# Rows by SyncE for five tiles a head, a re-ordered start and another last part in a graph and memory kernel

## The chip, the cores and the metric

The kernel runs on one core of one Trainium2 chip. The metric is device microseconds (us) of one execution. The engines are TensorE (PE in the profile, its weight loads PEld), VectorE (DVE), ScalarE (ACT), GpSimd (POOL) and SyncE (SP); they run side by side and meet at semaphores.

## The reference

Input is x (2048 x 128) and a symmetric adjacency matrix (2048 x 2048). Four blocks follow each other, each on the layer-normalised x and added to it:

```
x = x + hyperbolic_graph_attention(norm(x), adj)      # dense masked softmax over 2048 neighbours
x = x + lns_linear(norm(x))                           # sign(x w) * |x| @ |w| + bias
x = x + graph_attention(norm(x), adj)                 # the second attention: leaky scores, elu
x = x + product_key_memory_attention(norm(x))         # 8 heads
```

The last block takes most of the time. For each of the 8 heads and each of the 2048 rows: two queries of 64 are compared with 128 keys each, the best 16 of each are combined to the best 16 of their sums, and these 16 numbers pick 16 rows of a table of 8 x 16384 rows (a key and a value of 128 floats each, so 1 KB a row). The 16 rows are summed with softmax weights: k and v of that row. Then comes causal attention over the 2048 rows, softmax(q k^T) v, and a projection added to x:

```
k = einsum(kv_scores, keys_table[ind]); v = einsum(kv_scores, values_table[ind])
attn = softmax(where(causal, q @ k.T, -max)); out = (attn @ v) @ Wo
```

All of it is float32.

## The kernel before

The 2048 rows are 16 tiles of 128. The three first blocks are done by about 340 us; their last part, the second attention, ends in five groups of tiles, GROUPS = (0,2), (2,6), (6,10), (10,14), (14,16). Of each group VectorE makes the ELU (elu_in and elu_out, with ScalarE's elu_exp between), adds it to x and takes the variance, ScalarE the root (norm_root), VectorE the normalising factors (normal), ScalarE the normalised rows (rows_in), TensorE their transposes (group), ScalarE their copy to aT (group_out). Before the change groups 3 and 4 end after TensorE's sum of tile 0 of head 0, and ScalarE does elu_exp(3) and all the rest of the two groups behind kv_out(0), the copy of that sum. Only then come project(5), scores(0) and step 1.

The memory block is a loop over heads (0, a hardware loop for 1 to 6, and 7) and in it over steps t = 0 to 15. Work of several tiles is in flight in a step:

- VectorE finds the 16 best of tile t+4 (find_start to look_up_5; the row numbers go to `rows`, rows_full), spreads the weights of tile t+1 to 16 diagonal matrices (spread, line 792), takes the maxima of tile t-1's scores (score_max, L799) and adds tile t-2's projected output to x (add_out, L807 and L812).
- GpSimd gathers tile by tile (gather, L321): one indirect DMA for each k of 0 to 15, which brings one table row to each of 128 partitions, into slot t % 4 of `ring`. Before a tile it waits for rows_full and for slot_free (L319), which ScalarE gives when the tile four before is summed (L1175).
- SyncE fetches the sixteenth rows (k = 15) of the tiles for which by_rows holds; GpSimd then issues 15 gathers for such a tile. The row numbers are transposed by TensorE (turn_offsets), scaled and copied by ScalarE (offsets_out) to `offs`, and SyncE loads them to registers 32 at a time (L268) and issues 128 DMAs of 1 KB (L272). Before, these are tiles 3, 7, 11, 15 (without 3 in head 0), and the offsets of tile t+3 are turned in step t.
- TensorE, in step t: project(t+5) (L1589 to L1593), the offsets, sums(t) (L1565: 16 products of a diagonal matrix with 128 x 256 gathered rows, waiting for four landings at a time), then values(t-1) (L1628 transposes of the probabilities, L1641 products with v, L1658 projection), turn_keys(t) (L1597) and scores(t) (L1610 past columns, L1616 and L1617 own columns).
- ScalarE makes the exponentials of the scores (softmax, L1248), copies transposed probabilities (L1259), sums (L1177), keys (L1268) and outputs (L1263).

Each engine's order is written out by hand; there is no planner. In the last step of head 7 the kernel before splits tile 15's sum around the first scores (sums(..., (0,)), then (1, 2), then the last quarter inside values(14)), has the maximum in two parts (L943, L946), and ends with softmax(15) over 2048 columns and values(15). The last addition is L954, and SyncE copies the last three tiles out.

## Time and profile before

| what | us |
|---|---|
| median of 3 runs | 2843.3 |
| lowest and highest of them | 2838.46, 2846.46 |
| the profiled execution, its own time | 2838.24 |
| its span, first to last instruction | 2836.3 |
| mean granted TensorE clock in it | 0.932 of full |

The profile is of one execution. Times in a timeline are us from the start of the span; a row is a start, a duration, the engine, the line, the operation, what it writes and reads, and in square brackets how long the engine sat idle before it and what ended that. DVEq, ACTq, PEq and POOLq are the engines' queues, here waits on semaphores. "issue" means that nothing in the profile shows a wait.

### The profile page before, as it was taken

The page shows a single profiled execution, that of the slowest core. Times are in us where ns is not written, and L with a number is a line of the kernel's source. Part 1 is how long each engine was busy: PE and PEld are TensorE (multiplying, and loading weights), DVE is VectorE, ACT ScalarE, POOL GpSimd, SP SyncE. Part 2 cuts the span into 40 slices and gives each one's busy share as a digit, 9 for nine tenths or more (in the row PEclk, how much of TensorE's full clock was granted, in tenths as well). Part 3 has the DMA queues.
Part 4 walks back from the last instruction along what each step waited for, and adds up shares of the span by engine and source line. Part 5 has one row for each costly group of instructions (what it writes and reads, how often), then busy time and mean ns, then how long its engine had stood idle before and what let it go on. Part 6 is the DMA issues. An engine that isn't in the chain of part 4 may idle for free. (4 is left out here: it accounts for less than half of the span.)

```text
span 2836.3 us, 47902 instructions
## 1 busy us (share of the span) xinstructions
PE 2195.5 (77%) x11489; PEld 1773.8 (63%) x11489; DVE 1867.1 (66%) x6336; ACT 783.3 (28%) x2063; POOL 1931.2 (68%) x2033
## 2 busy tenths in 40 slices
PE   6948678887788777886878767877788777877777
PEld 6948556766566556665666655665566655665565
DVE  6689777766666666657566665656666666666541
ACT  5746422221122212221222212221223112221222
POOL 0003767777777777777777777777777777777773
PEclk8969889999999899999899899998999989989999
DMA  4301333333333333333333333333333333333332
GB/s 154 108 1 30 91 95 108 111 108 108 107 111 108 109 108 111 107 108 109 107 110 109 109 107 111 109 110 107 108 110 108 109 108 110 108 109 107 107 108 74
DMA packets 116173, 293.47 MB, mean 103 GB/s; under 512 B 37600, under 2 KB 49248, under 8 KB 113792
## 3 DMA queue, kind: packets, MB, share of 16 engines
q0 software_dynamic: 96816, 264.50, 32.6%
q1 hardware_dynamic: 14880, 23.22, 2.5%
q10 hardware_dynamic: 4144, 2.17, 0.3%
q8 instruction: 105, 1.72, 0.3%
q14 instruction: 228, 1.87, 0.2%
HBM read 288.69 MB, written 1.05 MB: 102 GB/s over the span
## 5 line engine op out<-in xcount | busy, mean ns | idle before, releaser
L321 POOL DMA_INDIRECT ring<-table,rows x2017 | 1923.6, 954 | 707.4 <-issue 578.3
L1565 PE MATMUL ps<-ring,staged 128*128 128x256 f32 x4096 | 995.8, 400 | 191.0 <-DMA ring<-table,rows 169.8
L1565 PEld LDWEIGHTS ps<-ring,staged 128*128 128x128 f32 x4096 | 806.0, 200 | 355.4 <-DMA ring<-table,rows 212.1
L807 DVE RECIPROCAL prec<-psum_row 128x1 f32<-128x1 f32 x128 | 21.0, 164 | 502.1 <-DVEq L806 501.8
L1641 PE MATMUL ps<-s2w,work 128*128 128x128 f32 x2176 | 306.2, 288 | 34.6 <-PEq L1639 33.8
L1177 ACT ACTIVATE work<-ps 128x256 f32<-128x256 f32 x128 | 49.0, 383 | 978.6 <-ACTq L1175 978.6
L1641 PEld LDWEIGHTS ps<-s2w,work 128*128 128x128 f32 x2176 | 274.3, 198 | 64.7 <-issue 61.2
L1610 PE MATMUL ps<-work,qT 128*128 128x512 f32 (+3 forms) x576 | 242.8, 552 | 70.4 <-PEq L1602 67.0
L799 DVE TENSOR_REDUCE nmax<-ps 128x1 f32<-128x128 f32 (+7 forms) x127 | 162.7, 1281 | 204.2 <-DVEq L798 203.5
L792 DVE TENSOR_TENSOR staged<-ps,wgt 128x2048 f32<-128x2048 f32 x128 | 292.0, 2281 | 0.2 <-issue 0.2
L1628 PE MATMUL ps<-ident,work 128*128 128x128 f32 x1088 | 189.8, 298 | 41.9 <-PEq L1551 21.7
L1610 PEld LDWEIGHTS ps<-work,qT 128*128 128x128 f32 x576 | 102.8, 195 | 178.8 <-issue 178.8
L1259 ACT ACTIVATE s2w<-ps 128x512 f32<-128x512 f32 (+2 forms) x320 | 169.4, 533 | 133.6 <-ACTq L1258 132.1
L1628 PEld LDWEIGHTS ps<-ident,work 128*128 128x128 f32 x1088 | 144.0, 154 | 79.1 <-issue 67.6
L1248 ACT ACTIVATE work<-ps,nmax 128x128 f32<-128x128 f32 (+15 forms) x128 | 148.3, 1158 | 39.2 <-ACTq L1246 34.7
L1593 PE MATMUL ps<-keyd,qpk 128*128 128x256 f32 x246 | 88.6, 444 | 88.9 <-PEq L1592 88.9
L762 DVE TENSOR_TENSOR pick<-bposf,ps 128x864 f32<-128x864 f32 x128 | 135.0, 1054 | 9.8 <-issue 0.4
L766 DVE TENSOR_TENSOR pick<-pick,ps 128x864 f32<-128x864 f32 x128 | 135.0, 1055 | 9.6
L1418 PE MATMUL ps<-work 128*128 128x128 f32 x1024 | 137.5, 279 | 4.1 <-PEq L1415 4.0
L1418 PEld LDWEIGHTS ps<-work 128*128 128x128 f32 x1024 | 126.7, 195 | 6.2 <-issue 6.0
L1658 PE MATMUL ps<-wo,oT 128*128 128x128 f32 x256 | 60.1, 317 | 87.3 <-PEq L1657 87.3
L1238 ACT ACTIVATE qpk<-ps 128x128 f32<-128x128 f32 x123 | 34.1, 277 | 333.1 <-ACTq L1237 333.1
(246 smaller groups left out, 2583.3 us busy)
## 6 DMA issues: line engine op xcount, KB each, us to landing
ring<-table SPq DMA_DIRECT2D x3968, 1.0 KB
ring<-table,rows POOLq DMA_INDIRECT x2017, 2.7
staged<-adj_in SPq DMA_DIRECT2D x16, 1024.0 KB, 4.8
xs<-x_in SPq DMA_DIRECT2D x4, 256.0 KB, 6.6
wpkq<-w_pkq ACTq DMA_DIRECT2D x7, 128.0 KB
out<-xs SPq DMA_DIRECT2D x1, 832.0 KB, 4.8
keyd<-pk_keys ACTq DMA_DIRECT2D x14, 32.0 KB
wo<-w_o ACTq DMA_DIRECT2D x7, 64.0 KB, 2.0
```

The lines of the kernel that those rows point to most:

```text
L321: nc.gpsimd.indirect_dma_start(ring[:, t % RING, k, :], None, table_d, bass.IndirectOffsetOnAxis(ap=rows[:, t % ROWS, k:k + 1], axis=0),). ...
L762: v.tensor_tensor(pick[:, :, :], bposf[:, :].unsqueeze(2).to_broadcast([P, TOPK, NCAND]), iota_ps.unsqueeze(1).to_broadcast([P, TOPK, NCAN ...
L766: v.tensor_tensor(pick[:, :, :], pick[:, :, :], cand_ps.unsqueeze(1).to_broadcast([P, TOPK, NCAND]), ALU.mult)
L792: v.tensor_tensor(diag(t), ident_ps.unsqueeze(1).to_broadcast([P, TOPK, P]), wgt[:, t % 4, :].unsqueeze(2).to_broadcast([P, TOPK, P]), ALU ...
L799: v.reduce_max(nmax[:, t % 2:t % 2 + 1], ps[:, 4:8, :].rearrange("p b n -> p (b n)")[:, 0:(t + 1) * P], X, negate=True).then_inc(nmax_full, 1)
L1248: s.activation(prob[:, t % 2, 0:L], ps[:, 4:8, :].rearrange("p b n -> p (b n)")[:, 0:L], ACT.Exp, bias=nmax[:, t % 2:t % 2 + 1], accum_out ...
L1259: s.activation(pts[:, (parity + b) % 2, 0:n * P], ps[:, 2 + (parity + b) % 2, 0:n * P], ACT.Copy).then_inc(pt_sb, 1)
L1418: ins = m.matmul(ps[:, OUT_BANKS[layer][t % banks], 0:D], ptg[:, n % 3, i * P:(i + 1) * P], hB[:, j, :], start=(j == 0), stop=(j == T - 1))
L1565: ins = m.matmul(to, diag(t)[:, k, :], ring[:, t % RING, k, :], start=(k == 0), stop=(k == TOPK - 1))
L1610: ins = m.matmul(ps[:, 4 + at // 512, 0:w], qT[:, t % 8, :], kT[:, at:at + w], start=True, stop=True)
L1628: ins = m.transpose(ps[:, 2 + (parity + b) % 2, j % 4 * P:(j % 4 + 1) * P], prob[:, t % 2, j * P:(j + 1) * P], ident[:, :])
L1641: ins = m.matmul(ps[:, 1, 0:P], kv[:, j, D:2 * D], pts[:, (parity + b) % 2, j % 4 * P:(j % 4 + 1) * P], start=(j == 0), stop=(j == t))
```

## The change

- by_rows: tiles 1, 4, 7, 10, 13 of each head (in head 0 only those above 4: 7, 10, 13). The offsets have three buffers, and the landings three semaphores, taken in turn. The offsets of tile a are turned in step a-3, as before. Tile 15's sixteenth row is a gather with a semaphore of its own.
- Opening: ScalarE does elu_exp(3) and exp_best(3) ahead of kv_out(0), then project_out(5) and key_out(0), and the rest of groups 3 and 4 after these. TensorE does project(5), turn_keys(0), scores(0) ahead of group(3), group(4). VectorE does find_halves(4) and then elu_out(3), find_all(4), and has spread(1) ahead of elu_out(4). Step 0 of head 0 is written out so.
- End of head 7: TensorE's loop stops at tile 13. Tiles 14 and 15 are summed by VectorE (weighted), row by row as the quarters land, with the running sum in PSUM. Row 15's softmax has two parts: columns 0 to 1919 with their own maximum, summed and projected as an output of its own, and the 128 own columns with the overall maximum; the first part is scaled by exp of the difference of the two maxima. The outputs are copied out in three parts: tiles 0 to 13, 14, 15.

The core of the diff:

```
-LOADED = 32
+LOADS = ((0, 32), (32, 64), (64, 96), (96, P))
+BY_ROWS = (1, 4, 7, 10, 13)
+def turned_at(t, first, last):
+    a = t + AHEAD - 1
+    return by_rows(a % T, first and a < T) and not (last and a >= T)
 def by_rows(t, first):
-    return t % RING == RING - 1 and not (first and t == RING - 1)
+    return t in BY_ROWS and not (first and t <= AHEAD)
+def buffer_of(t):
+    return BY_ROWS.index(t) % 3
...
-            def fetch_rows():
+            def fetch_rows(t):
+                for lo, hi in LOADS:
                     _, at = nc.values_load_multi_w_load_instructions(
-                        offs[0:1, c:c + LOADED], engines=(mybir.EngineType.SP,), min_val=0, max_val=(HEADS * NKV - 1) * ROW_BYTES,
+                        offs[0:1, buffer_of(t), lo:hi], engines=(mybir.EngineType.SP,), min_val=0, max_val=(HEADS * NKV - 1) * ROW_BYTES,
                         skip_runtime_bounds_check_because="row numbers are sums of a head's offset and two positions")
-                    for i in range(LOADED):
-                        sp.dma_start(ring[c + i:c + i + 1, RING - 1, TOPK - 1, :].bitcast(U8),
-                                     table_bytes[:, bass.ds(at[i], ROW_BYTES)]).then_inc(rows_in_sem, 16)
+                    for i in range(lo, hi):
+                        sp.dma_start(ring[i:i + 1, t % RING, TOPK - 1, :].bitcast(U8),
+                                     table_bytes[:, bass.ds(at[i - lo], ROW_BYTES)]).then_inc(copied_in[buffer_of(t)], 16)
...
+                    ).then_inc(last_in if t == T - 1 and k == TOPK - 1 else gathered[t % RING][k // QK], 16)
...
+            spread(1)
+            elu_out(4)
             weigh(AHEAD - 1)
...
+            def weighted(t, q):
+                landed(t, q)
+                for k in range(q * QK, (q + 1) * QK):
+                    w, row = wgt[:, t % 4, k:k + 1], ring[:, t % RING, k, :]
+                    if t == T - 1 and k == TOPK - 1:
+                        dve.wait_ge(last_in, 16 * HEADS)
+                    if k == 0:
+                        v.tensor_scalar(end_ps, row, w, None, ALU.mult)
+                    elif k < TOPK - 1:
+                        v.scalar_tensor_tensor(end_ps, row, w, end_ps, ALU.mult, ALU.add)
+                    else:
+                        v.scalar_tensor_tensor(kv[:, t, :], row, w, end_ps, ALU.mult, ALU.add).then_inc(kv_full, 1)
+                    v.drain()
+            def add_out(t):
+                add_out_1(t)
+                v.drain()
+                add_out_2(t)
+                v.drain()
+            for t in range(T - 2):
                 step(t, False, True)
+            add_out(T - 4)
+            weighted(T - 2, 0)
+            score_max(T - 3)
+            for q in range(1, QUARTERS):
+                weighted(T - 2, q)
+            score_max(T - 2)
+            add_out(T - 3)
+            dve.sem_inc(out_ready, 1)
+            weighted(T - 1, 0)
             dve.wait_ge(s_full, 1)
             dve.sem_inc(s_full, -1)
-            v.reduce_max(npart[:, 0:1], ps[:, 4:7, :].rearrange("p b n -> p (b n)"), X, negate=True)
+            v.reduce_max(max_past, ps[:, 4:8, :].rearrange("p b n -> p (b n)")[:, 0:(T - 1) * P], X,
+                         negate=True).then_inc(nmax_full, 1)
+            weighted(T - 1, 1)
+            weighted(T - 1, 2)
+            add_out(T - 2)
+            dve.sem_inc(out_ready, 1)
+            weighted(T - 1, 3)
             dve.wait_ge(s_full, 1)
             dve.sem_inc(s_full, -1)
-            v.reduce_max(npart[:, 1:2], ps[:, 7, :], X, negate=True)
+            v.reduce_max(max_own, ps[:, 7, 3 * P:4 * P], X, negate=True)
             v.drain()
-            v.tensor_tensor(nmax[:, 1:2], npart[:, 0:1], npart[:, 1:2], ALU.min).then_inc(nmax_full, 1)
-            add_out_1(T - 2)
+            v.tensor_tensor(max_all, max_past, max_own, ALU.min).then_inc(nmax_full, 1)
+            dve.wait_ge(scales_ok, 1)
+            v.scalar_tensor_tensor(denom, sum_past, old_scale, sum_own, ALU.mult, ALU.add)
             v.drain()
-            add_out_2(T - 2)
-            add_out_1(T - 1)
+            v.reciprocal(f_own, denom)
             v.drain()
-            v.scalar_tensor_tensor(xs[:, T - 1, :], ps[:, 1, P:2 * P], prec[:, 3:4], xs[:, T - 1, :],
+            v.tensor_tensor(f_past, f_own, old_scale, ALU.mult)
+            v.drain()
+            dve.wait_ge(proj_full, 1)
+            dve.sem_inc(proj_full, -1)
+            v.scalar_tensor_tensor(xs[:, T - 1, :], ps[:, 1, P:2 * P], f_past, xs[:, T - 1, :], ALU.mult, ALU.add)
+            v.drain()
+            dve.wait_ge(proj_full, 1)
+            dve.sem_inc(proj_full, -1)
+            v.scalar_tensor_tensor(xs[:, T - 1, :], ps[:, 0, P:2 * P], f_own, xs[:, T - 1, :],
                                    ALU.mult, ALU.add).then_inc(out_ready, 1)
...
+            def last_steps():
+                t = T - 1
+                past = t * P
+                row = prob[:, t % 2, :]
+                scored = ps[:, 4:8, :].rearrange("p b n -> p (b n)")
+                softmax(t - 2)
+                turned_out(t - 2, PARITY[t - 2], t - 1)
+                softmax(t - 1)
+                turned_block(t - 1, PARITY[t - 1], 0)
+                turned_block(t - 1, PARITY[t - 1], 1)
+                act.wait_ge(nmax_full, 1)
+                act.sem_inc(nmax_full, -1)
+                s.activation(row[:, 0:past], scored[:, 0:past], ACT.Exp, bias=max_past, accum_out=sum_past).then_inc(prob_full, 1)
+                turned_block(t - 1, PARITY[t - 1], 2)
+                turned_block(t - 1, PARITY[t - 1], 3)
+                output_turned()
+                for b in range(4):
+                    turned_block(t - 1, PARITY[t], b)
+                key_out(t, ps[:, 0, 2 * P:3 * P])
+                output_turned()
+                act.wait_ge(nmax_full, 1)
+                act.sem_inc(nmax_full, -1)
+                s.activation(row[:, past:N], scored[:, past:N], ACT.Exp, bias=max_all, accum_out=sum_own).then_inc(prob_full, 1)
+                s.activation(old_scale, max_past, ACT.Exp, scale=-1.0, bias=max_all).then_inc(scales_ok, 1)
+                act.wait_ge(pt_full, 1)
+                act.sem_inc(pt_full, -1)
+                s.activation(ptown[:, :], ps[:, 0, 3 * P:4 * P], ACT.Copy).then_inc(pt_sb, 1)
+                output_turned(oTown, ps[:, 0, 0:P])
...
+            project_out(AHEAD + 1)
+            key_out(0)
+            norm_root(*GROUPS[3])
+            rows_in(3)
+            elu_exp(4)
+            group_out(3)
+            norm_root(*GROUPS[4])
+            rows_in(4)
+            group_out(4)
+            for t in range(1, T):
...
+            def last_steps():
+                t = T - 2
+                exponentials()
+                past_scores(t)
+                values(t - 1, PARITY[t - 1], bank1, key=t)
+                t = T - 1
+                exponentials()
+                past_scores(t).then_inc(s_full, 1)
+                values(t - 1, PARITY[t - 1], bank1)
+                exponentials()
+                turn_block(t - 1, PARITY[t], 0, t)
+                bank1()
+                for b in range(3):
+                    turn_block(t - 1, PARITY[t], b + 1, t)
+                    sum_block(t - 1, PARITY[t], b)
+                kv_copied()
+                turn_keys(t, ps[:, 0, 2 * P:3 * P])
+                sum_block(t - 1, PARITY[t], 3).then_inc(ot_full, 1)
+                pe.wait_ge(kt_sb, 1)
+                pe.sem_inc(kt_sb, -1)
+                own_scores(t)
+                output(t)
+                exponentials()
+                m.transpose(ps[:, 0, 3 * P:4 * P], prob[:, t % 2, t * P:N], ident[:, :]).then_inc(pt_full, 1)
+                pe.wait_ge(pt_sb, 1)
+                pe.sem_inc(pt_sb, -1)
+                m.matmul(ps[:, 0, 0:P], kv[:, t, D:2 * D], ptown[:, :], start=True, stop=True).then_inc(ot_full, 1)
+                pe.wait_ge(ot_sb, 1)
+                pe.sem_inc(ot_sb, -1)
+                m.matmul(ps[:, 0, P:2 * P], oTown[:, :], wo[:, :], start=True, stop=True).then_inc(proj_full, 1)
...
+            project(AHEAD + 1)
+            kv_copied()
+            turn_keys(0)
+            scores(0)
+            group(3)
+            group(4)
+            pe.wait_ge(bank7_free, 1)
+            pe.sem_inc(bank7_free, -1)
+            for t in range(1, T):
```

## Rows read from the trace of the kernel before

**Rows 1.** The page, busy us (share of the span) and instructions
```profile
PE 2195.5 (77%) x11489; PEld 1773.8 (63%) x11489; DVE 1867.1 (66%) x6336; ACT 783.3 (28%) x2063; POOL 1931.2 (68%) x2033
```
**Rows 2.** Line L321: engine, operation, durations, first and last start
```profile
L321 POOL DMA_INDIRECT ring<-table,rows x2017: 940/946/2411, 255.6 to 2801.6; - x184
...
DMA to landing us min/median/max: 2.6/2.7/5.0
```
**Rows 3.** Timeline, GpSimd: start, duration, instruction, idle before
```profile
371.87 0.95 POOL L321 DMA_INDIRECT ring<-table,rows  x1 [0.30 <-issue]
...
380.83 0.94 POOL L321 DMA_INDIRECT ring<-table,rows  x1 [8.02 <-POOLq L319]
...
2801.59 0.94 POOL L321 DMA_INDIRECT ring<-table,rows  x1 [0.30 <-issue]
```
**Rows 4.** Timeline of the opening, all engines
```profile
331.71 9.39 PE L1565 MATMUL ps<-ring,staged 128*128 128x256 f32 x32 [3.86 <-PEq L1558]
...
342.36 0.69 DVE L583 SCALAR_TENSOR_TENSOR fin<-fin,work 128x512 f32<-128x512 f32 x1 [7.44 <-DVEq L345]
...
351.91 0.17 DVE L779 CAST rows<-rowf 128x16 uint32<-128x16 f32 x1
...
355.09 1.09 PE L1459 MATMUL ps<-ident,work 128*128 128x128 f32 x4 [13.99 <-PEq L1457]
...
362.32 0.66 PE L1459 MATMUL ps<-ident,work 128*128 128x128 f32 x2 [6.14 <-PEq L1457]
...
367.73 0.30 DVE L710 MAX8 half<-sim 128x8 f32<-128x128 f32 x1 [0.88 <-DVEq L708]
...
368.79 0.64 PE L1589 MATMUL ps<-aT,wpkq 128*128 128x128 f32 x2
...
371.56 8.19 PE L1565 MATMUL ps<-ring,staged 128*128 128x256 f32 x32
...
379.76 0.17 DVE L779 CAST rows<-rowf 128x16 uint32<-128x16 f32 x1
...
379.95 0.38 ACT L1177 ACTIVATE work<-ps 128x256 f32<-128x256 f32 x1 [7.32 <-ACTq L1175]
```
**Rows 5.** SyncE: line L268, and one fetch in the timeline
```profile
L268 SPq TENSOR_LOAD <-offs x124: 2025/2124/2153, 413.3 to 2775.4; - x124
...
934.92 48.30 SPq L272 DMA_DIRECT2D ring<-table  x128
```
**Rows 6.** Windows: stretch, length, busy us, granted clock, DMA share, GB/s
```profile
500.00:1500.00 1000.00, 791.20 (x3914) 625.66 (x3915) 657.68 (x2318) 238.07 (x664) 756.21 (x801) 0.95 0.38 109
```
**Rows 7.** Timeline of the end, all engines
```profile
2765.65 1.99 PE L1565 MATMUL ps<-ring,staged 128*128 128x256 f32 x8 [1.36 <-DMA ring<-table,rows]
...
2778.05 2.02 DVE L799 TENSOR_REDUCE nmax<-ps 128x1 f32<-128x1792 f32 x1 [3.55 <-DVEq L798]
...
2795.81 3.25 PE L1610 MATMUL ps<-work,qT 128*128 128x512 f32 x8 [0.56 <-PEq L1602]
...
2799.65 2.16 DVE L799 TENSOR_REDUCE nmax<-ps 128x1 f32<-128x1920 f32 x1 [3.76 <-DVEq L798]
...
2801.94 1.86 ACT L1248 ACTIVATE work<-ps,nmax 128x1920 f32<-128x1920 f32 x1 [6.27 <-ACTq L1246]
...
2804.03 5.16 PE L1610 MATMUL ps<-work,qT 128*128 128x512 f32 x8 [2.81 <-PEq L1621]
...
2818.44 0.30 PE L1597 MATMUL ps<-ident,work 128*128 128x128 f32 x1 [0.74 <-PEq L1551]
...
2819.29 0.46 PE L1616 MATMUL ps<-causal,ident 128*128 128x128 f32 x2 [0.55 <-PEq L1649]
...
2825.59 1.06 PE L1628 MATMUL ps<-ident,work 128*128 128x128 f32 x8 [1.49 <-PEq L1621]
...
2832.12 0.28 ACT L1263 ACTIVATE oT<-ps 128x128 f32<-128x128 f32 x1 [1.41 <-ACTq L1262]
...
2833.39 0.35 DVE L954 SCALAR_TENSOR_TENSOR xs<-ps,prec,xs 128x128 f32<-128x128 f32 x1
```

More of the change, by code:

```diff
@@ L835, in step @@
                 a = (t + AHEAD) % T
-                begun = not (first and t == 0)
-                find = begun and not (last and t >= T - AHEAD)
+                find = not (last and t >= T - AHEAD)
                 out = not (first and t < 2)
-                weigh = begun and not (last and t >= T - AHEAD + 1)
+                weigh = not (last and t >= T - AHEAD + 1)
                 if t == T - AHEAD and find:
@@ L853, in step @@
                     find_second(a)
-                if begun:
-                    score_max((t - 1) % T)
-                if not (last and t == T - 1):
+                score_max((t - 1) % T)
+                if not (last and t == T - 3):
                     spread((t + 1) % T)
@@ L938, in _, with landed, per @@
                     step(t, False, False)
-            for t in range(T):
-                step(t, False, True)
+            def landed(t, q):
+                def per(first):
+                    return [16 * (QK - (q == QUARTERS - 1 and (s == T - 1 or by_rows(s, first)))) for s in range(t % RING, T, RING)]
+                dve.wait_ge(gathered[t % RING][q], (HEADS - 2) * sum(per(False)) + sum(per(True)) + sum(per(False)[:t // RING + 1]))
+            def weighted(t, q):
[11 more added lines that the diff above has]
+                    v.drain()
@@ L1315, in _ @@
                     step(h, t, False, False)
-            for t in range(T):
+            for t in range(T - 2):
                 step(HEADS - 1, t, False, True)
-            softmax(T - 1)
-            turned_out(T - 1, PARITY[T - 1])
+            last_steps()
         @block.tensor
@@ L1537, in per @@
                 def per(first):
-                    return [16 * (QK - (q == QUARTERS - 1 and by_rows(s, first))) for s in range(t % RING, T, RING)]
+                    return [16 * (QK - (q == QUARTERS - 1 and (s == T - 1 or by_rows(s, first)))) for s in range(t % RING, T, RING)]
                 if first:
@@ L1572, in _ @@
             bank1()
-            sums(0, 0, range(QUARTERS), True)
-            group(3)
-            group(4)
-            pe.wait_ge(bank7_free, 1)
-            pe.sem_inc(bank7_free, -1)
+            sums(0, 0, True)
             def project(t):
@@ L1668, in step @@
                     project((t + AHEAD + 1) % T)
-                if t % RING == 0 and not (first and t == 0):
+                if turned_at(t, first, last):
                     turn_offsets()
-                if first and t == 0:
-                    kv_copied()
-                    turn_keys(0)
-                    scores(0)
-                    return
-                if last and t == T - 1:
-                    sums(h, t, (0,), False, end_ps)
-                    exponentials()
-                    past_scores(t).then_inc(s_full, 1)
-                    sums(h, t, (1, 2), False, end_ps)
-                    values(t - 1, PARITY[t - 1], bank1, t)
-                    return
                 if t == 0:
@@ L1687, in step @@
                     bank1()
-                    sums(h, 0, range(QUARTERS), False)
+                    sums(h, 0, False)
                     kv_copied()
@@ L1692, in step @@
                         bank1()
-                    sums(h, t, range(QUARTERS), first)
+                    sums(h, t, first)
                     exponentials()
```

173 lines of the change are left out of this document (85 added, 88 removed).

## Prediction

> **What bounds the kernel now.** I read the busy shares first, then the largest group, then its instructions in order of time, then the two ends of that stretch. The busy shares [rows 1] name no engine: TensorE 77%, GpSimd 68%, VectorE 66%. The group of gathers [rows 2] is the one to follow: 2017 of them, one every 1.25 us (0.95 busy, 0.30 before the next), from 255.6 to 2801.6 us. In order of time [rows 3], gather 80 starts at 371.87, gather 81 at 380.83 after 8.02 us of waiting, and the last at 2801.59. From the 81st to the last are 1936 steps in 2420.76 us, 1.2504 us each, so GpSimd never waits there: that stretch is its queue and nothing else, whatever the other engines do. TensorE's waits inside it are waits for gathers. So the time has three parts: the opening up to gather 81, the stretch at 1.25 us per gather, and the end from the last gather on (2801.59 to 2836.3), which is a chain over TensorE, ScalarE and VectorE [rows 7]. The DMA engines are at a share of 0.38 [rows 6], so issuing, not moving, sets the 1.25.
>
> **Part 1, rows fetched by SyncE.** Before, head 0 has 3 tiles of which the sixteenth row goes by SyncE (7, 11, 15), the other seven 4 each: 31. After, head 0 has 7, 10, 13, the others 1, 4, 7, 10, 13: 3 + 35 = 38. So 7 gathers less: 7 x 1.2504 = 8.75 us, if GpSimd stays the bound. All removed ones lie behind gather 81. The cover: SyncE needs 48.3 us for its 128 copies with three loads of row numbers between, and 2.1 us for the first load [rows 5], 50.4 us. Before, a fetch comes every 63 gathers, 79 us; after, 3 tiles apart, 47 gathers, 58.8 us, so 8 us are left. Five fetches are 252 us of a head of 251 gathers, 313.9 us. The fetch of tile a still starts in step a-3 and is wanted after the last quarter of tile a; between lie about 62 gathers less the 12 us by which that step starts late (tile 13's scores end 12 us after its last quarter starts [rows 7]), 65 us against 50.4 plus the landing. At tile 4 it is tight, because TensorE comes out of a head's first step late and catches up: there it may wait a few us, but the ring holds four tiles, 60 us of gathers, so GpSimd doesn't notice. Bounds: 0 (something else takes over) and 8.75; I take 8.75. The added order of offsets (a buffer of three, one transpose and one copy per fetch, as before) makes 7 more of each on engines with idle time: nothing.
>
> By the Trainium skill (DMA: Bandwidth & Descriptors, "Issuing engines are not separate DMA queues") DMAs of all engines end on the same 16 DMA engines, and issuing from several saves only the issuing engine's time; were the transfers the bound, this part would give 0 and the sum 20.3 instead of 29. This case's trace shows issue as the bound: even steps at a share of 0.38.
>
> **Part 2, the opening.** Gather 81 is tile 5's first. It wants tile 5's row numbers (VectorE ends them at 379.93) and slot 1, free when tile 1 is summed (ScalarE copies it at 379.95) [rows 4]: both are late, and equally. Both go back to one place. TensorE ends tile 0's sum at 341.1 and then sits 13.99 us until VectorE and ScalarE have group 3's normalised rows, does group 4 at 362.32, and only then project(5), scores(0), project(6) (368.79) and tile 1's sum (371.56 to 379.75). VectorE in turn had waited 7.44 us for ScalarE's exponential of group 3, queued behind the copy of tile 0's sum; from there to tile 4's row numbers took it 342.36 to 352.08, 9.7 us. After the change that exponential is ahead of the copy, so these 9.7 us start when the halves of tile 4 are searched, about 335.0 (an estimate: tile 0's spread ends near 331.7, and the search takes some 3 us), and end at 344.8. TensorE does project(5) and scores(0) at once, by about 345.6 (two copies and four products at the 0.4 us that each takes with its handover [rows 7], 4.5 us), and ScalarE then turns to group 3's root. From tile 4's row numbers to group 3's transposes were 3.2 us (351.91 to 355.09), so these come at 348.0 to 348.8; from group 3's to group 4's 7.2, now with spread(1) between but done while ScalarE writes group 3's rows: 355.2 to 356.0. The copy takes 0.85 with its handovers, project(6) 2.8 and tile 1's sum 8.2 to 9.4: slot 1 is free at 367.9 to 369.1. VectorE enters step 1 when group 4's rows are normalised, about 354.5, and ends tile 5's row numbers 12.2 us later (367.73 to 379.93 before), 366.7. GpSimd wants both at 371.87 + 1.25 = 373.1. The wait goes with 4 us to spare: 8.96 - 1.25 = 7.71 us. What is late next: tile 6, wanted 20 us later at 393, with TensorE's step of about 14 us behind 369; later tiles have more room. Bounds 0 and 7.71; I take 7.71.
>
> Together the last gather starts at 2801.59 - 8.75 - 7.71 = 2785.13.
>
> **Part 3, the end.** I count from the start of the last gather. Before, the last VectorE operation ends at 2833.74, that is at +32.15 [rows 7]. After, tiles 14 and 15 are no longer summed by TensorE, so nothing waits for their last gathers but VectorE, which adds 16 rows of 256 columns one after another. The nearest row is the same operation over 128 columns, 0.35 us; 128 more columns at about 1 ns (the reductions: 2.16 - 2.02 = 0.14 us for 128) make 0.49, with 0.07 between, 0.56 us, and 2.2 us a quarter (between 1.4 and 4).
> The chain starts with tile 13's scores. Tile 13 has 15 gathers now and tile 15 has 16, and the wait of 1.36 us before its last quarter goes, so its row maximum starts at -24.9 instead of -23.5. From there:
> maximum 2.0; softmax 1.75 (1.86 over 1920 columns) with its accumulator and two handovers, 2.2; scores of row 14 over 14 tiles. These take 3.0 at the full clock (3.25 x 14/15), but TensorE has then idled 4.2 us; before, it idled 2.8 us and the 3.25 us of work took 5.16. So 4.9, reached at -15.8. Two blocks of row 13's values, 3.7 (16 tiles take 6.5 from the first transpose to the copy of the result, 0.41 a tile, and the start of the first); tile 14's keys and own scores 1.8, to -10.3; the sum of tile 14 is ready at -15.0 (last landing -17.2, then 2.2), in time. Rest of row 13's values and the copy 3.4, softmax 14 2.1, scores of row 15 3.4: to -1.4. Maximum of 1920 columns 2.2, its exponential 2.2 to +3.0. This exponential stands on ScalarE before the last two blocks of row 14, so these end late: copies, sums, copy and projection to 6.9. Then 15 tiles of row 15's values: 6.7, to 13.6. Own scores 0.7, to 14.3, and from there ten short operations in a row (maximum, minimum, exponential, its partner, transpose, copy, product, copy, projection, last addition) at 0.43 to 0.5 (a transpose and a copy take 0.85 from start to start of the next), 4.6: +18.9. Tile 15's sum is no part of it: VectorE does its last quarter behind add_out(14), at 7.6 to 9.8, wanted at 12.4.
> The exponential in the middle gives TensorE another idle of about 1.3 us (2.9 if it slips), which the trace doesn't price alone: between 0 and 1.9 us more. I take 0.7: +19.6. Gain 32.15 - 19.6 = 12.5 us, between 8 (every idle costs 1.9, VectorE at 1 us per row) and 15.
> The Trainium skill (TensorE: Matmul & The Clock Gate, "HAM oscillation") says that idle gaps between bursts put TensorE back to the lower clock, which speaks against taking sums off TensorE here. The trace agrees: 5.16 us against 3.25 after the 2.81 us gap. With no such drop the forecast would be 2.6 us lower.
>
> **The sum.** Last operation at 2785.13 + 19.6 = 2804.7. The last copy out and what follows took 2836.3 - 2833.74 = 2.56: span 2807.3. The profiled execution's own time is 1.94 over its span: 2809.2, 29.0 us (1.0%) under its 2838.24. That execution is 5.1 under the median of the runs; I take 29.0 off the median: 2814.3.
>
> **Rivals.**
> A. The opening's wait stays or comes back at tile 6 or 7, because VectorE and ScalarE in the new order trail by more than the 4 us to spare. For it: both releasers of gather 81 must move, through some ten handovers. Against: both have room. Price 7.7: 2822. Chance 0.12.
> B. The end gives half or less: TensorE at the lower clock through the chain, or the exponential over 1920 columns in the middle pushing two more waits. Price 6 to 9: 2822. Chance 0.17.
> C. Other side: SyncE becomes the bound. It is then busy 80% of a head, with 8 us between fetches where it had 28. The point where it decides is a fetch of 313.9 / 5 = 62.8 us; every us above costs 35 us (5 x 7). At 65 us: 77 us over, so 2814 + 77 = 2891; slower than before from 63.6. For it: its copies already follow each other without a gap (128 in 48.3 us, loads included). Against: nothing of this burst depends on how often it comes, and the DMA engines have room. Chance 0.04.
> D. The seven gathers bring nothing, because the bytes are the same and the DMA engines, or TensorE waiting for rows at tile 4 in each head, set the pace. Against: a DMA share of 0.38, and 60 us of ring. Price 8.75: 2823. Chance 0.05.
> The forecast itself 0.62.
>
> **The numbers.** 2814, range 2804 to 2828: the low end is the end's best (15) and a run at the lower edge of the three shown, the upper A or D with B's lower price (2814 + 7.7 + 6 = 2828). A measurement of this kernel tells about 0.3%, 8.5 us, from no change. All cases but C are over that; a mixture of A, B and D at their worst (25 us) is what lands within it. Faster 0.94, same 0.02, slower 0.04.
>
> **What would show it.** 2010 gathers; no wait of GpSimd of a microsecond or more from gather 36 on, the 81st at 373.1; the last starting at 2785; its pace still 1.25; SyncE's bursts still 48 us, about 10 apart. At the end: no sum of tile 14 or 15 on TensorE in head 7, row 13's maximum 25 us before the last gather, a granted clock of half in row 14's scores, the last VectorE operation 19 to 20 us behind the last gather. The forecast is wrong if GpSimd shows waits inside the stretch, or if the last operation is over 24 us behind the last gather.

## The result, and the profile after

The changed kernel takes 2813.39 us (median of four runs, 2812.64 to 2815.2) where the kernel before takes 2842.07 (2838.46 to 2846.46): a ratio of 0.9899 with a 95% interval from 0.9882 to 0.9917. The prediction was 2814. The profiled execution took 2812.64 us, with a span of 2810.8.

The page of the changed kernel, busy us with the share of the span [rows 1]:

```profile
PE 2187.1 (78%) x11434; PEld 1761.3 (63%) x11434; DVE 1878.3 (67%) x6369; ACT 785.3 (28%) x2073; POOL 1930.2 (69%) x2026
```

Its gathers (now line L340), and what their engine waited for, in us and times [rows 2]:

```profile
L340 POOL DMA_INDIRECT ring<-table,rows x2010: 945/949/2422, 254.9 to 2790.7; - x183
  issue: 577.2, 1892
  POOLq L338: 116.6, 100
```

Seven gathers fewer. L338 is the wait for a slot of the ring. The timeline of GpSimd around the gather that had waited 8.02 us [rows 3], and its last gather:

```profile
372.78 0.95 POOL L340 DMA_INDIRECT ring<-table,rows  x1 [0.31 <-issue]
...
2790.74 0.95 POOL L340 DMA_INDIRECT ring<-table,rows  x1 [0.30 <-issue]
```

Gather 81 starts at 372.78 without a wait (forecast 373.1). But 2790.74 is 5.6 us later than the forecast 2785.13: 1929 steps in 2417.96 us are 1.2535 each, not the 1.2504 of before, which is 6.0 us. The pace is the same while SyncE copies and while it doesn't (1.2535 and 1.2534), and the duration of one gather is up by the same 3 ns: median 949 against 946 [rows 2].

The end of the changed kernel in the timeline, all engines [rows 7], in which the last gather starts at 2790.74:

```profile
2765.80 2.02 DVE L818 TENSOR_REDUCE nmax<-ps 128x1 f32<-128x1792 f32 x1 [1.28 <-DVEq L817]
2767.74 4.42 DVE L969 SCALAR_TENSOR_TENSOR ps<-ring,wgt,ps 128x256 f32<-128x256 f32 x8
2769.94 5.52 PE L1701 MATMUL ps<-work,qT 128*128 128x512 f32 x8 [4.29 <-PEq L1712]
...
2785.43 3.46 PE L1701 MATMUL ps<-work,qT 128*128 128x512 f32 x8 [1.38 <-PEq L1712]
...
2789.03 2.16 DVE L993 TENSOR_REDUCE tail<-ps 128x1 f32<-128x1920 f32 x1 [1.94 <-DVEq L992]
2791.32 1.86 ACT L1348 ACTIVATE work<-ps,tail 128x1920 f32<-128x1920 f32 x1 [0.78 <-ACTq L1347]
...
2799.60 0.48 DVE L971 SCALAR_TENSOR_TENSOR work<-ring,wgt,ps 128x256 f32<-128x256 f32 x1
2801.86 0.27 PE L1688 MATMUL ps<-ident,work 128*128 128x128 f32 x1
...
2807.53 0.35 DVE L1018 SCALAR_TENSOR_TENSOR xs<-ps,tail,xs 128x128 f32<-128x128 f32 x1 [1.46 <-DVEq L1017]
```

From the last gather to the end of the last VectorE operation are 17.14 us, where before had 32.15 and the forecast 19.6. A row added on VectorE takes 0.49 us with 0.07 before the next (eight take 4.42). Tile 15's sum is ready at 2800.08 and wanted at 2801.86, so it hides, with 1.8 us to spare. The span of 2810.8 is the forecast 2807.3, plus 5.6 for the pace, less 2.5 for the end, and 0.4 in the last copy out.

### The profile page after: what moved, and what is told of

The parts are those of the page before. It is cut to its first block and busy times, and to the rows that moved or that the text cites. A ratio compares the mean times of both kernels' runs of the same rounds, so it can differ in the third digit from the quotient of the medians.

```text
span 2810.8 us, 49771 instructions
## 1 busy us (share of the span) xinstructions
PE 2187.1 (78%) x11434; PEld 1761.3 (63%) x11434; DVE 1878.3 (67%) x6369; ACT 785.3 (28%) x2073; POOL 1930.2 (69%) x2026
## 3 DMA queue, kind: packets, MB, share of 16 engines
HBM read 288.69 MB, written 1.05 MB: 103 GB/s over the span
## 5 line engine op out<-in xcount | busy, mean ns | idle before, releaser
L340 POOL DMA_INDIRECT ring<-table,rows x2010 | 1922.6, 957 | 699.3 <-issue 577.2
L1309 ACT ACTIVATE work<-ps,nmax 128x128 f32<-128x128 f32 (+7 forms) x127 | 146.1, 1151 | 22.2 <-ACTq L1307 21.5
```

The costliest lines, as they stand in the source:

```text
L340: nc.gpsimd.indirect_dma_start(ring[:, t % RING, k, :], None, table_d, bass.IndirectOffsetOnAxis(ap=rows[:, t % ROWS, k:k + 1], axis=0),). ...
L1309: s.activation(prob[:, t % 2, 0:L], ps[:, 4:8, :].rearrange("p b n -> p (b n)")[:, 0:L], ACT.Exp, bias=nmax[:, t % 2:t % 2 + 1], accum_out ...
```

## The experiments

Kernels of one group ran on one chip beside the kernel before. In the first and the third group everything ran in a slow condition of the machine (the kernel before at 4200 and 4108 us instead of 2836), in which a change of one per cent can't be judged, and the decisive kernels of the first were run again in the second.

**First group: the kernel before and the changed one again, and two parts undone.** b_again and a_again have no edit. u1_four has four fetched tiles a head, four tiles apart as before, though not the same ones (before: 3, 7, 11, 15):

```
-BY_ROWS = (1, 4, 7, 10, 13)
+BY_ROWS = (1, 5, 9, 13)
```

u2_open has the old order of the opening on all three engines and everything else new; TensorE's part of it:

```
             group(3)
+            group(4)
...
-            project(AHEAD + 1)
-            kv_copied()
-            turn_keys(0)
-            scores(0)
-            group(4)
+            project(AHEAD + 1)
+            kv_copied()
+            turn_keys(0)
+            scores(0)
```

> The kernel before, once more, for its pace only. Between gather 81 and the last its gathers were 1.2504 us apart, those of the changed kernel 1.2535, which cost that one 6.0 us of the 8.75 that seven gathers less should bring. Theory A (the pace is the chip's and the execution's, not the kernel's): before and after have the same pace here, within 0.001, whatever it is. Theory B (SyncE's seven further fetches slow every gather): before again 1.2504, after again 1.2535.

> The changed kernel, once more. Theory A: the same pace as before in this call, within 0.001; the last gather then starts 16.1 us before the one of before (8.75 + 7.71, less the 0.4 that its first gathers differ), and the time is 31 to 32 us under before. Theory B: 1.2535 against 1.2504, and 28 to 29 us under. Both: last VectorE operation 17.1 us behind the last gather's start.

> The changed kernel with four tiles a head by SyncE (1, 5, 9, 13), three in head 0: 2017 gathers as before, the rest as changed. Theory A: 8.75 us slower than the changed kernel, same pace as it. Theory B: seven gathers more but each 0.0031 us faster: 2.8 us slower only, pace 1.2504.

> The changed kernel with the opening of before (groups 3 and 4 ahead of project(5) and scores(0), ScalarE's exponential of group 3 behind the copy of tile 0's sum, spread(1) last). Both theories: gather 81 waits some 8 us again, everything behind it 7.7 us later, time 7.7 us over the changed kernel. If the wait was going to be made good later (rival: work that the ring's four slots hide anyway), under 2 us.

Measured: before 4199.62 us (4176.14 to 4208.09), b_again 4190.19. a_again 4482.67, ratio 1.0672 [1.0618, 1.0727]; u1_four 4291.82, 1.0239 [1.0189, 1.0288]; u2_open 4505.25, 1.0728 [1.0672, 1.0783]. None of the times expected came: the change is 6.7% slower here, and with four fetches a head instead of five it is slower by 4.3 points less. What did come is theory A of b_again: where gathers follow each other without a wait they are 1.2502 us apart in b_again and 1.2501 in a_again. So the changed kernel isn't what made the pace 1.2535 in its first profile. The waits of GpSimd in a_again, in us, times and the longest:

```profile
POOL ring L340 <- POOLq L338: 1748.6, 126, 84.2
POOL ring L340 <- issue: 574.7, 1884, 0.9
```

The issue row is as ever, the other 1632 us more than in the first profile: GpSimd is no longer the bound. Nor is it in the kernel before, where this wait is 1327.2 us in b_again. SyncE's copies in a_again (ns min/median/max):

```profile
L289 SPq DMA_DIRECT2D ring<-table x4864: 2/228/1436, 467.6 to 4424.5; - x195
```

The median copy takes what it takes otherwise, but some take 1.4 us, and the 128 copies of a fetch come to some 77 us alone and 98 us when three fetches follow each other (294 us for three), against 48.7. The kernel before has the same long ones (maximum 1421 ns), and its other engines stand too, at fixed lines: the wait before one VectorE operation, which is 9.4 us in the first profile of before, in b_again:

```profile
L752 DVE MAX8 best<-candr 128x8 f32<-128x54 f32 x128 | 27.9, 218 | 357.6 <-issue 355.5
```

Nothing that the profile shows releases these waits. What causes them I can't settle.

How far SyncE holds up the rest can be read from TensorE's wait for the fetched sixteenth row, on the semaphore of the copies (L1661, in the kernel before L1564; us, times, longest), in a_third of the second group (undisturbed), in b_again, u1_four, a_again, and in c1_all and s7_seven of the third group (six and seven fetches a head):

```profile
PE ps L1662 <- PEq L1661: 2.7, 2, 2.1
...
PE ps L1565 <- PEq L1564: 161.3, 10, 24.0
...
PE ps L1662 <- PEq L1661: 200.5, 12, 25.3
...
PE ps L1662 <- PEq L1661: 319.1, 15, 25.2
...
PE ps L1662 <- PEq L1661: 567.0, 24, 40.8
...
PE ps L1662 <- PEq L1661: 1036.8, 45, 43.1
```

In the slow condition TensorE waits for rows of SyncE already before the change, and 158 us more in the changed kernel, of the 303 us by which the span of a_again (4491.5) is over b_again's (4188.2). With seven fetches it waits 875 us more, and the span of 4991.5 is 803 over b_again's, 886 over the median of before in its own group (4105.5).

**Second group: the same comparison undisturbed.** a_third is the changed kernel, u1_four_b and u2_open_b are u1_four and u2_open. u3_end has the new rows and opening with the old end: TensorE sums tiles 14 and 15 (in parts, as before), row 15's maximum has two parts and its exponential is one over 2048 columns, and tile 15's sixteenth row is a gather. Its edit is the end of three engines and the two last copies out put back; the core:

```
-            add_out(T - 4)
-            weighted(T - 2, 0)
-            score_max(T - 3)
...
-            weighted(T - 1, 3)
+            v.reduce_max(npart[:, 0:1], ps[:, 4:7, :].rearrange("p b n -> p (b n)"), X, negate=True)
...
+            v.reduce_max(npart[:, 1:2], ps[:, 7, :], X, negate=True)
```

> The changed kernel once more, since the chip of the first call ran every kernel at 4180 us and more: there SyncE took 98 us for the 128 copies of a fetch instead of 48, over the 62.8 us from which the prediction's rival C has it decide. Theory A (C's rule: the changed kernel wins where a fetch stays under 62.8 us and loses where it doesn't): fetches of 48 to 49 us go with 28 to 32 us under before, fetches of about 98 us with 5 to 8% over it. Theory B (the second chip slows the changed kernel for another reason): the sign doesn't follow the length of a fetch.

> The changed kernel with four tiles a head by SyncE (1, 5, 9, 13), three in head 0: 2017 gathers. Where a fetch takes 48 us: 8.75 us slower than the changed kernel if the pace per gather is the chip's (theory A), 2.8 us if seven fetches more had slowed every gather from 1.2504 to 1.2535 (theory B). Where a fetch takes 98 us: 4 to 5% faster than the changed kernel.

> The changed kernel with the opening of before. Where a fetch takes 48 us: gather 81 waits some 8 us, everything behind it comes 7.7 us later, 7.7 us over the changed kernel; rival (made good later): under 2 us. Where a fetch takes 98 us: within 0.5% of the changed kernel, since GpSimd isn't the bound there.

> The changed kernel with the end of before (TensorE sums tiles 14 and 15, row 15's softmax in one part over 2048 columns), tile 15's sixteenth row still a gather of GpSimd. Where a fetch takes 48 us: 13 to 16 us slower than the changed kernel (its last operation came 17.1 us behind the last gather's start, before's 32.1, and one gather more stands at the end here); rival (the gain of the end came from the idle chip and not from the order): under 6 us. Same last gather start as the changed kernel in both theories.

Measured, beside the kernel before at 2835.64 us (2835.04 to 2839.65, seven runs):

| kernel | us | ratio, 95% | gathers | gather 81 | last gather | end of last operation behind it |
|---|---|---|---|---|---|---|
| a_third | 2806.95 | 0.9894, 0.9877 to 0.9910 | 2010 | 373.83 | 2785.75 | 17.69 |
| u1_four_b | 2814.80 | 0.9922, 0.9905 to 0.9938 | 2017 | 372.78 | 2793.62 | 17.50 |
| u2_open_b | 2817.31 | 0.9930, 0.9913 to 0.9946 | 2010 | 381.39 | 2793.44 | 19.70 |
| u3_end | 2818.78 | 0.9937, 0.9920 to 0.9953 | 2010 | 373.85 | 2785.82 | 27.98 |

The time of each kernel over a_third is what the part is worth: 7.85 us for the seven gathers, 10.4 for the opening, 11.8 for the end. Their sum is 30.0, against the whole change's 28.7: the parts add up to within 1.3 us. The 11.8 are under the 13 to 16 that were expected of u3_end, which had been counted from before's 32.1 and the 17.1 of the first profile of the changed kernel; they are well over the rival's 6. In the two profiles u3_end is 10.3 us longer behind its last gather, and the rest is in the copies out and between executions. In u1_four_b gather 81 happens to start 1.05 earlier, and from there it has 1936 steps to a_third's 1929, 8.9 us more. The group of gathers of u1_four_b and of a_third, and what GpSimd waited for in a_third:

```profile
L340 POOL DMA_INDIRECT ring<-table,rows x2017: 942/946/2409, 255.0 to 2793.6; - x184
```

```profile
L340 POOL DMA_INDIRECT ring<-table,rows x2010: 942/946/2417, 256.1 to 2785.8; - x183
  issue: 576.7, 1892
  POOLq L338: 117.0, 105
```

The wait on L338 is 117.0 us in 105 cases; before had 124.5 in 105 ones: only the opening's wait has gone, and none has come. With the old opening it is back, and moves every later gather; GpSimd in u2_open_b:

```profile
372.07 0.95 POOL L340 DMA_INDIRECT ring<-table,rows  x1 [0.30 <-issue]
381.39 0.94 POOL L340 DMA_INDIRECT ring<-table,rows  x1 [8.37 <-POOLq L338]
```

The other 2.0 us by which u2_open_b is longer behind its last gather have rows of their own: the scores of rows 14 and 15, in u2_open_b (line L1699), in a_third and in u1_four_b:

```profile
2772.73 6.28 PE L1699 MATMUL ps<-work,qT 128*128 128x512 f32 x8 [4.29 <-PEq L1710]
...
2788.97 5.16 PE L1699 MATMUL ps<-work,qT 128*128 128x512 f32 x8 [1.38 <-PEq L1710]
```

```profile
2765.11 5.92 PE L1701 MATMUL ps<-work,qT 128*128 128x512 f32 x8 [4.29 <-PEq L1712]
...
2780.99 3.46 PE L1701 MATMUL ps<-work,qT 128*128 128x512 f32 x8 [1.38 <-PEq L1712]
```

```profile
2773.86 4.94 PE L1701 MATMUL ps<-work,qT 128*128 128x512 f32 x8 [4.29 <-PEq L1712]
...
2788.76 3.46 PE L1701 MATMUL ps<-work,qT 128*128 128x512 f32 x8 [1.38 <-PEq L1712]
```

The same work after the same idle time takes 4.94 to 6.28 us in row 14, and 3.46 or 5.16 in row 15. In the windows of row 15's scores (of u2_open_b and of a_third; the last three numbers are the granted clock, the DMA share and GB/s) the clock was 0.66 and 1.00:

```profile
2789.00:2794.00 5.00, 5.00 (x9) 2.13 (x10) 1.46 (x3) 0.00 (x0) 3.78 (x5) 0.66 0.94 277
```

```profile
2781.00:2784.40 3.40, 3.40 (x10) 1.65 (x11) 1.47 (x3) 0.00 (x0) 2.59 (x3) 1.00 0.96 266
```

So the idle of 1.38 us costs 0 or 1.7 us. The prediction held 0.7, between 0 and 1.9. Of the four undisturbed profiles with the new end, three are without it. That it goes by the execution and not by the kernel is seen in a_again: the changed kernel itself, with 5.06 us here. The idle of 2.8 us ahead of row 15's scores in the old end is no different: 5.16 in the profile of before [rows 7], but 3.46 in u3_end and in b_again.

The end of u3_end is 27.98 us long, where the profile of before had 32.15 [rows 7] with the same order of work. The start of tile 14's last quarter and the transposes behind it, first in the kernel before, then in u3_end, here with the start of row 14's scores (2795.81 in before [rows 7]):

```profile
2785.63 2.45 PE L1565 MATMUL ps<-ring,staged 128*128 128x256 f32 x8 [2.55 <-DMA ring<-table,rows]
2787.87 2.03 PE L1628 MATMUL ps<-ident,work 128*128 128x128 f32 x8
```

```profile
2768.56 2.00 PE L1592 MATMUL ps<-ring,staged 128*128 128x256 f32 x8 [1.03 <-DMA ring<-table,rows]
2770.39 0.60 PE L1647 MATMUL ps<-ident,work 128*128 128x128 f32 x4
...
2777.56 3.25 PE L1632 MATMUL ps<-work,qT 128*128 128x512 f32 x8 [0.55 <-PEq L1624]
```

Counted from the last gather, the quarter starts at -15.96 and -17.26, which is 1.3 us: it waits for tile 14's last landing, and behind that tile come 15 gathers in before and 16 here, since tile 15's sixteenth row is now a gather; from there to row 14's scores are 10.2 and 9.0 us, the same instructions, at a granted clock of 0.66 and 1.00 in their first 4.4 us, after 2.55 and 1.03 us of idle; and row 15's scores took 5.16 us before [rows 7] and 3.46 here, 1.7 more. That makes 4.2 in all, the whole difference: 1.3 belong to tile 15's one gather more, 2.9 to the clock.

**Third group: is the end's clock worth more, and SyncE's limit.** w1_warm puts nine products of which nothing is used between row 13's values and the wait for row 14's exponential, so that TensorE doesn't stand idle. a1_order has ScalarE do the last two blocks of row 14 ahead of row 15's exponential. s7_seven fetches seven tiles a head by SyncE, c1_all six and has both edits above.

```
 # w1_warm, TensorE, ahead of the exponentials' wait
+                for i in range(9):
+                    m.matmul(ps[:, 3, 0:2 * P], ident[:, :], kv[:, i, :], start=True, stop=True)
 # a1_order, ScalarE: these two from behind row 15's exponential to ahead of it
+                turned_block(t - 1, PARITY[t - 1], 2)
+                turned_block(t - 1, PARITY[t - 1], 3)
 # s7_seven
+BY_ROWS = (0, 2, 4, 6, 8, 10, 12)
 # c1_all
+BY_ROWS = (0, 2, 5, 7, 10, 12)
```

> The changed kernel with 9 products of the identity and 256 columns, written to a free PSUM bank and never read, in TensorE's 4.3 us of waiting before row 14's scores. Theory A (the half clock there costs what the prediction says): the scores take 3.0 instead of 5.5 us, the last operation comes 14.6 to 15.4 us behind the last gather's start instead of 17.1 to 17.7. Theory B (the scores hide behind another engine): under 0.5 us earlier. The last gather's start doesn't move.

> The changed kernel with ScalarE's copies of the last two blocks of row 14's probabilities ahead of row 15's exponential over 1920 columns. Theory A (the exponential in the middle holds up TensorE, as the prediction's sum has it): last operation 0.7 to 1.3 us earlier, at 16.0 to 16.8. Theory B (VectorE's additions or the bank's release bind there): no change within 0.3 us.

> The changed kernel with seven tiles a head by SyncE (0, 2, 4, 6, 8, 10, 12; four in head 0): 1992 gathers, 249 a head, 311 us of GpSimd, and seven fetches of about 51 us, 356 us, of SyncE. Rival C's rule (a head lasts as long as the slower of the two queues): a head of 356 us, 42 more than the changed kernel's 314, so 290 us over it, about 3100, on a chip with fetches of 48 to 49 us. Rival rule (SyncE's copies can be late because the ring hides them): 22 us under the changed kernel. On a chip with fetches of 98 us: some 700 us a head.

> Six tiles a head by SyncE (0, 2, 5, 7, 10, 12; four in head 0), and both edits of the end (TensorE kept busy, ScalarE's order). 2002 gathers, 250 a head, 312.6 us; six fetches, 305 us: by rival C's rule still GpSimd's. The last gather starts 10.0 us earlier than in the changed kernel, the last operation comes 13.5 to 14.5 behind it: 12 to 14 us under the changed kernel. If SyncE, with 8 us a head to spare, already binds: fetches without gaps, waits of GpSimd, and a time over the changed kernel's. On a chip with fetches of 98 us: 14 to 20% over the changed kernel.

Measured, beside before at 4107.52 us (4092.06 to 4125.65) on the chip of the second group: w1_warm 4389.75, ratio 1.0671 [1.0627, 1.0715]; a1_order 4381.09, 1.0648 [1.0596, 1.0700]; c1_all 4615.30, 1.1232 [1.1181, 1.1283]; s7_seven 4990.27, 1.2138 [1.2087, 1.2190]. The changed kernel wasn't run in this group (in the first it was at 1.0672), and the times expected for an undisturbed chip couldn't be tested. What was expected of the slow condition was too much: s7_seven's heads take some 593 us and not 700, and c1_all is 5% over w1_warm and a1_order and not 14 to 20% over the changed kernel. (s7_seven has 1995 gathers, where its expectation counted 1992: of 56 places 53 are fetched.) The row of w1_warm against that of a1_order, which has no filler (timeline, then the window of the scores, of w1_warm and then of a1_order):

```profile
4353.49 4.05 PE L1759 MATMUL ps<-work,ident 128*128 128x256 f32 x18
4357.95 3.25 PE L1701 MATMUL ps<-work,qT 128*128 128x512 f32 x8 [0.41 <-PEq L1712]
```

```profile
4358.00:4361.20 3.20, 3.20 (x10) 1.66 (x11) 2.83 (x6) 0.00 (x0) 0.00 (x0) 1.00 0.00 0
```

```profile
4339.81 6.19 PE L1701 MATMUL ps<-work,qT 128*128 128x512 f32 x8 [4.29 <-PEq L1712]
```

```profile
4339.80:4346.00 6.20, 6.19 (x10) 2.90 (x11) 3.90 (x8) 0.00 (x0) 0.00 (x0) 0.52 0.01 3
```

With the filler the engine is idle 0.41 us instead of 4.29, is granted 1.00 (2.4 GHz) instead of 0.52 (nearly all of it at 1.2 GHz), and the eight products take 3.25 us instead of 6.19. On an undisturbed chip the same row is 4.94 to 6.28, so the filler should bring 1.7 to 3.0 us there, an estimate.

The end can be compared even so, because the stalls stop with the gathers: a_again's last gather starts at 4411.0 and its row 13's maximum at 4443.85, and from there to row 14's scores are 4.14 us, as in the undisturbed profiles. From the start of that maximum (us):

| profile | to row 15's scores | to the end of the last operation |
|---|---|---|
| changed kernel, first profile | 19.63 | 42.08 |
| a_third | 20.02 | 42.47 |
| a_again | 20.10 | 44.07 |
| w1_warm (filler) | 17.35 | 40.01 |
| a1_order (order) | 20.30 | 45.73 |
| c1_all (both) | 17.35 | 38.99 |

The other profiles with the new end and no edit of it are at 41.41 to 44.55 in the last column. So the scores don't hide behind another engine (theory B of w1_warm): the filler brings row 15's scores 1.7 to 3.0 us nearer in both profiles that have it, and the end 1.4 us or more. The order of ScalarE isn't settled: from row 15's scores to the end c1_all has 21.64 and w1_warm 22.66, 1.0 less as theory A says, but a1_order 25.43 and a_again 23.97; in a1_order TensorE idles longer there and eight products of row 15's values take 1.92 us instead of 1.09. In time none of this was shown: the executions of w1_warm are 20 us apart. Nor is it known what six or seven fetches would bring where SyncE isn't stalled. No version was shown to beat the changed kernel.

## Why the prediction was right

**What bounds the kernel.** GpSimd's queue, as read: with seven gathers less the kernel ends 7.85 us earlier, and gather 81 held up by 7.6 us moves the last gather by 7.7. Neither would hold if another engine set the pace. Rival D (the gathers bring nothing, price 8.75) is refuted by u1_four_b.

**Part 1,** 8.75 predicted: 7.85 in time, 8.9 in the distance from gather 81 to the last. The copies of a fetch take 48.7 us, as expected. They aren't spread evenly, 10 us apart, as the prediction had it: three follow each other in head 0 (402.5 to 553.4 us in a_third) and two in each later head, and the other gaps are 3 to 26 us. But from head 1 on a slot is free 33 us or more before its gather (30 before), so it cost nothing.

**Part 2,** 7.71 predicted: 7.6 to 7.7 from the wait, 10.4 in the time of the undone kernel. In its profile 7.7 lie before the last gather, 2.0 are the clock in the end, and 1.5 the last copy out; its other executions have no profile. The order of events in a_third, timeline of the opening [rows 4]:

```profile
335.62 0.69 DVE L602 SCALAR_TENSOR_TENSOR fin<-fin,work 128x512 f32<-128x512 f32 x1 [0.19 <-DVEq L364]
...
345.18 0.17 DVE L798 CAST rows<-rowf 128x16 uint32<-128x16 f32 x1
...
348.44 1.09 PE L1555 MATMUL ps<-ident,work 128*128 128x128 f32 x4 [3.47 <-PEq L1553]
...
354.30 0.66 PE L1555 MATMUL ps<-ident,work 128*128 128x128 f32 x2 [4.76 <-PEq L1553]
...
358.67 8.07 PE L1662 MATMUL ps<-ring,staged 128*128 128x256 f32 x32
...
365.33 0.17 DVE L798 CAST rows<-rowf 128x16 uint32<-128x16 f32 x1
...
366.95 0.38 ACT L1241 ACTIVATE work<-ps 128x256 f32<-128x256 f32 x1 [7.21 <-ACTq L1239]
```

VectorE's wait for the exponential is 0.19 us where it was 7.44. Group 3's transposes come at 348.44 (forecast 348.0 to 348.8), group 4's at 354.30 (355.2 to 356.0), tile 5's row numbers at 365.50 (366.7), and slot 1 is copied at 366.95 (free at 367.9 to 369.1). GpSimd wants both at 373.8, so 6.5 us are to spare, not 4. Rival A (the wait stays, 7.7) didn't come, neither here nor at tile 6.

**Part 3,** a gain of 12.5 predicted: 15.0 and 14.5 in the two profiles of the changed kernel, from before's 32.15, and 11.8 in time by the undone kernel. The two differ because 1.3 us of the gain come from tile 15's one gather more, behind which everything is counted, and stay in u3_end, and 2.9 from the clock, which was poor in the one profile of before that all of the forecast was counted from (0.66 and 0.67 in two stretches where u3_end has 1.00). By the two profiles that differ in the end alone, u3_end and a_third, the new order is worth 10.3 us and not 12.5, with the same 3.46 us in row 15's scores. Against +19.6 the first profile is 2.5 us shorter: 0.6 are there by the end of row 15's exponential (+2.5 instead of +3.0), 0.9 come in the 15 tiles of row 15's values (5.8 us from the projection's end instead of 6.7), 0.7 were the allowance for a second clock drop that didn't fall, and the rest is in the short operations. Mis-sized the other way is the drop in row 14's scores: 4.9 forecast, 4.94 to 6.28 measured.

Three readings of it were wrong and cost little. The 3.25 us [rows 7] are row 14's scores themselves, with 14 tiles, so their length at the full clock is 3.25 and not 3.25 x 14/15 = 3.0, as w1_warm shows; and the 5.16 have 15 tiles, 3.46 at the full clock, so the drop in them is 1.7 and not 1.9. The wait of 1.36 us before tile 13's last quarter didn't go (1.69 in the first profile): row 13's maximum is at -24.9 as forecast mainly because one gather more follows. And that 2.8 us of idle cost anything at all was the draw of one profile (3.46 in u3_end and b_again), while the 4.29 us of the new order cost something in all nine profiles of it without filler.

The Trainium skill's rule (TensorE: Matmul & The Clock Gate, "HAM oscillation"), that idle gaps put the engine back to its lower clock, is borne out for the long gap: 6.19 us after 4.29 us idle, 3.25 with filler between, at a granted clock of 0.52 and 1.00. The gaps of 1.38 and 2.8 us cost 1.6 to 1.7 us in some profiles and nothing in others. Rival B took this and an exponential that pushes two more waits for up to 9 us; the drop in row 14's scores cost 1.7 to 3.0 and 1.9 of it were in the sum, the exponential pushed nothing. The Trainium skill (DMA: Bandwidth & Descriptors, "Issuing engines are not separate DMA queues"), which the prediction weighed, says that issuing from another engine saves only the issuer's time; here the issuer is the bound, and this is worth all of 7.85 us.

**The total.** The gain forecast was 29.0 us, and the medians give 28.7 in both groups that ran undisturbed. That this is so near is partly luck: the first profile took 2812.64 us where 2809.2 were forecast for it, with a pace 3 ns a gather too slow (+6.0 us over 1929 gathers), which isn't the kernel's, and an end 2.5 us too short; the 5.1 us that the forecast of 2814.3 adds, because the profile of before lay that much under its median, covered the rest. The profile of a_third, at the pace of before, has its last gather at 2785.75 against 2785.13 forecast: parts 1 and 2 are right as they stand.

**Rival C,** the only one on the other side, said that SyncE becomes the bound above 62.8 us a fetch. Undisturbed a fetch with its first load takes 50.8 us and the change gains 1.1%; in the slow condition it takes 77 to 107 and the change loses 6.7%. The sign turned, but not by the rival's rule. The 62.8 are a fifth of an undisturbed head, and in the slow condition the heads of the kernel before take 484 us; the five fetches of a_again take 460 a head, so by the slower of the two queues nothing would be lost, and its heads take 525. SyncE is 88% busy there, and 95% with seven fetches (s7_seven). It holds the rest up before it is full: its rows come late for TensorE by 158 us more than in b_again, at most about half of the loss of 303. With four fetches (u1_four) the new order is still 2.4% slower than before, with 39 us of such waits in 97 us. In that condition the fifth fetch costs 4.3 points, and what costs the rest is open.

## What to carry to other kernels

Where one engine's queue of DMA issues is full from end to end and the DMA engines are not, each issue taken off it is worth its spacing, and each wait in it that nothing later absorbs is worth its length: find the first wait whose removal moves all that follow. Before work is put on a helper queue, divide the period by the helper's time per job: that ratio (here 62.8 to 50.8) is the reserve. It is no guarantee: in a worse condition a gain of 1% turned into a loss of 7% with the helper only 88% busy, so compare the time of the unchanged kernel first. Taking work off TensorE in a latency chain cost back some of it in clock here, and filler products in the gap kept the clock.

## What the runs showed of the hardware

The same kernel before took 2835.64 and 4107.52 us on the same chip at different times. In the profiles of before and b_again the first 255 us, up to the first gather, go alike; soon after, and as long as gathers run, all engines stand at times with nothing in the trace that they wait for (SyncE's copies for up to 1.4 us, VectorE before the operation shown for up to 6.5), and behind the last gather a_again and a_third go alike again. TensorE's mean granted clock is 0.77 to 0.79 in the kernel before, instead of 0.93. The cause is open.

GpSimd issues its gathers at one of two paces in an execution, some 1.2501 to 1.2505 us or 1.2531 to 1.2535 where one follows another without a wait (median duration 946 or 949 ns). It isn't the kernel: the changed kernel is at the second pace in its first profile and at the first in a_third and a_again, and the kernels u1_four and u2_open are at the second pace in the first group and at the first pace in the second. Over 1929 gathers this is 6 us, 0.2%, and a single profile's stretch can't be compared closer than that.
